# Two attention units' value products and output projections in one run, every second step, in a two-layer graph attention kernel

## The reference

```
# layer 0 (8 heads of 32)
nx = ln(x); q, k, v = nx @ wq + bq, nx @ wk + bk, nx @ wv + bv
scores = q k^T / sqrt(32) + where(adj > 0, 0.1 * adj * adj, -inf)
out = softmax(scores) v                       # the value products
x1 = x + (out @ wo + bo)                      # the output projection
y = x1 + gelu(ln(x1) @ w1 + b1) @ w2 + b2
# layer 1
q, k, v = y @ Wq + bq, y @ Wk + bk, y @ Wv + bv
attn = softmax(where(adj == 0, -inf, q k^T / sqrt(32)))
h = attn v @ Wo + bo
out = ln(h + y) * gamma + beta
```

## Time and profile before

| | |
|---|---|
| median of 3 runs | 2196.2 us (2194.52 to 2197.47) |
| the profiled execution, its own time | 2197.36 us |
| its span, first to last instruction | 2195.3 us |
| TensorE busy | 98% of the span |
| VectorE, ScalarE, GpSimd busy | 82%, 77%, 53% |
| mean granted TensorE clock | 0.988 |

### The profile page before, as it was taken

The page is one execution under the profiler, slowest core; times in us unless marked ns, Lnnn a source line. Parts: engine busy times, 40 slices in busy tenths (PEclk is TensorE's granted clock), DMA queues, the critical chain, the costliest instruction groups (busy, mean ns, idle before and its releaser), DMA issues.

```text
span 2195.3 us, 58908 instructions
## 1 busy us (share of the span) xinstructions
PE 2150.0 (98%) x20300; PEld 1859.5 (85%) x20300; DVE 1802.1 (82%) x8414; ACT 1683.8 (77%) x5646; POOL 1155.7 (53%) x1266
## 2 busy tenths in 40 slices
PE   8899999999999999999999999999999999999986
PEld 6688888888888888888888888888888888888875
DVE  6688888888888888888888888888888888888774
ACT  5578787778777778877778877788877787877773
POOL 4345655445655455655455555455555455555454
PEclk9999999999999999999999999999999999999997
DMA  4010111011111001111101110101111001110000
GB/s 128 25 35 28 40 33 40 23 31 35 40 33 36 27 28 38 37 36 31 32 28 38 34 39 31 33 26 40 33 40 31 30 28 40 33 40 29 22 14 17
DMA packets 94309, 75.74 MB, mean 35 GB/s; under 512 B 8129, under 2 KB 93761, under 8 KB 94017
## 3 DMA queue, kind: packets, MB, share of 16 engines
q1 hardware_dynamic: 94016, 71.99, 10.7%
HBM read 55.20 MB, written 16.78 MB: 33 GB/s over the span
## 4 chain that ended last, share of the span: by engine, by line
PE 95%; DVE 2%; issue 1%; ACT 1%; POOL 0%; DMA 0%; SPq 0%; POOLq 0%; DVEq 0%
PE p_bank L1124 67%; PE p_heads L1221 10%; PE p_heads L1208 8%; PE p_bank L1240 7%; PE p_bank L1143 4%; ACT scores L650 1%; DVE normed L883 0%; DVE x_two L768 0%; DVE probs_t L920 0%; ACT normed L661 0%; DMA scores<-in_L_gnn_wk 0%; DVE scores L861 0%; DVE adj_c L814 0%; SPq L440 0%; POOL w_up L374 0%
## 5 line engine op out<-in xcount | busy, mean ns | idle before, releaser
L650 ACT ACTIVATE scores<-scores,negmax 128x128 f32<-128x128 f32 x2048 | 793.7, 393 | 25.4 <-DVE negmax L861 25.0
L585 POOL TENSOR_TENSOR scores<-scores,inverse 128x512 f32<-128x512 f32 x512 | 541.9, 1064 | 339.6 <-DVE inverse L872 339.6
L650 ACT ACTIVATION_READ_ACCUMULATOR scores<-scores,negmax 128x1 f32 x2048 | 392.2, 192 | 0.0
L1124 PEld LDWEIGHTS p_bank<-w_down,hidden 128*128 128x128 f32 x3072 | 374.7, 190 | 8.6 <-issue 6.0
L1124 PE MATMUL p_bank<-w_down,hidden 128*128 128x256 f32 x3072 | 381.8, 284 | 0.0
L1124 PE MATMUL p_bank<-normed,w_up 128*128 128x512 f32 x1536 | 370.3, 397 | 1.9 <-DVE normed L883 1.9
L1124 PEld LDWEIGHTS p_bank<-normed,w_up 128*128 128x128 f32 x1536 | 285.0, 189 | 67.6 <-issue 8.4
L1221 PE MATMUL p_heads<-ident,scores 128*128 128x128 f32 x2048 | 313.1, 276 | 8.3 <-DVE negmax L861 3.5
L861 DVE CUSTOM_DVE_ANT_0 scores<-p_heads,adj_a 128x128 f32<-128x128 f32 x1024 | 235.2, 286 | 43.7 <-issue 43.7
L1221 PEld LDWEIGHTS p_heads<-ident,scores 128*128 128x128 f32 x2048 | 241.2, 141 | 35.0 <-DVE negmax L861 11.1
L673 ACT ACTIVATE p_bank<-p_bank,ready_cols 128x512 f32<-128x512 f32 x256 | 169.5, 662 | 131.4 <-PE p_bank L1124 125.9
(11 more groups left out here) (117 smaller groups left out, 3704.5 us busy)
## 6 DMA issues: line engine op xcount, KB each, us to landing
res_a<-in_x SPq DMA_DIRECT2D x32, 512.0 KB, 3.8
out<-res_c SPq DMA_DIRECT2D x128, 128.0 KB, 1.7
x_in<-in_x SPq DMA_DIRECT2D x31, 512.0 KB, 3.8
adj_a<-in_adj SPq DMA_DIRECT2D x32, 256.0 KB, 2.9
adj_c<-in_adj SPq DMA_DIRECT2D x32, 256.0 KB, 2.9
piece_room<-in_L_gnn_w SPq DMA_DIRECT2D x2, 512.0 KB, 8.1
x_two<-in_x SPq DMA_DIRECT2D x1, 512.0 KB, 5.5
res_c<-in_L_gnn_w SPq DMA_DIRECT2D x1, 512.0 KB, 6.3
```

What stands on the lines that cost most here:

```text
L585: nc.gpsimd.tensor_tensor(rows_g, rows_g, inverse[:, step % 2, heads].unsqueeze(2).broadcast_to([P, HC, P]), ALU.mult).then_inc(probs_made, 1)
L650: last = nc.scalar.activation(scores[:, k % 2, h], scores[:, k % 2, h], ACT.Exp, scale=-1.0, bias=negmax[:, k % 2, h:h + 1], accum_out=tot ...
L1124: last = nc.tensor.matmul(dst, stationary(i), moving(j), start=(n == 0), stop=(n == total_n - 1))
```

## The change

V and W are made for two units at once, in the odd steps: step 1 takes the last two A units of the turn before, step 3 the first two C units, step 5 the last two C units, step 7 the first two A units. Even steps have no V and no W. `probs_t` and `heads_t` get two rooms each. The two units' evacuations are one instruction of double width (`heads_high`, `heads_low`, `add_residual`); `measure` takes two units with shared steps. Q, K and V are moved so that even steps have more of them. The norm of stage M's input is applied for units 0 and 1 in steps 0 and 1, for units 2 and 3 in step 2. The steps after the change:

The order within a step is the same as before on each engine. The core of the diff:

```
-        by_step[k] = ([("V", r - 2), ("W", r - 2)] if r >= 2 or pending else []) + (
+        pair = [(r - 3, r - 2)] if r % 2 and (r >= 3 or pending) else []
+        by_step[k] = [("V", units) for units in pair] + [("W", units) for units in pair] + (
             [("T", r - 1)] if r >= 1 or pending else [])
...
-        early = {1: ("Q", "A", 0), 2: ("V", "A", 0), 4: ("DOWN", 1), 6: ("Q", "C", 0), 7: ("V", "C", 0)}
+        early = {1: ("Q", "A", 1), 2: ("V", "A", 0), 4: ("DOWN", 1), 6: ("Q", "C", 0), 7: ("V", "C", 1)}
         mid = {0: [("K", "A", 0)], 3: [("UP", 0), ("UP", 1)], 5: [("K", "C", 0)]}
-        fill = {0: [("K", "A", 1)], 1: [("Q", "A", 1)], 2: [("V", "A", 1)],
+        fill = {0: [("K", "A", 1), ("Q", "A", 0)], 2: [("V", "A", 1)],
                 3: [("UP", j) for j in range(2, FC)] + [("DOWN", 0)],
-                5: [("K", "C", 1)], 6: [("Q", "C", 1)], 7: [("V", "C", 1)]}
+                5: [("K", "C", 1)], 6: [("Q", "C", 1), ("V", "C", 0)]}
...
-        probs_t = sb("probs_t", [P, H, P])
-        heads_t = sb("heads_t", [P, 2, KC, P], F32R)
+        probs_t = sb("probs_t", [P, 2, H, P])
+        heads_t = sb("heads_t", [P, 2, 2, KC, P], F32R)
...
-                nc.vector.tensor_tensor(x[:, b, :], p_bank[bank][:, 0:D], x[:, b, :], ALU.add
-                                        ).then_inc(drained[bank], 1)
+                x = residual[stage][:, b:b + len(units), :].rearrange("p g n -> p (g n)")
+                nc.vector.tensor_tensor(x, p_bank[bank][:, 0:len(units) * D], x, ALU.add).then_inc(drained[bank], 1)
...
-                    if k == 2:
-                        for r in s.late.get(k, []):
-                            apply_norm(t, r, GB - 1)
+                    if k == 2 and s.m and s.pending:
+                        normalize_m(t, 2, t.group_m, t.projections("A", 1))
+                        normalize_m(t, 3, t.group_m, t.projections("A", 1))
...
+            def value_products(t, units):
+
+                bank, dst = take(t, ("O", units))
+                u_last, stage, _ = t.unit(units[-1])
+                pe.wait_ge(turned_out0, u_last + 1)
+                pe.wait_ge(turned_out1, u_last + 1)
...
+                for i, r in enumerate(units):
+                    _, _, b = t.unit(r)
+                    for h in range(H):
+
+                        j, c = h % HC, h // HC
+                        last = nc.tensor.matmul(dst[HD * j:HD * (j + 1), (i * KC + c) * P:(i * KC + c + 1) * P],
+                                                values[room(t, stage)][:, b, h * HD:(h + 1) * HD],
+                                                probs_t[:, parity(r), slot_of(c, j), :], start=True, stop=True)
+                last.then_inc(filled[bank], 1)
+
+            def project(t, units):
+
+                bank, number = t.bank(("O", units))
+                pe.wait_ge(drained[bank], number)
+                bank, dst = take(t, ("W", units))
+                w = weight[weights_of[t.unit(units[0])[1]][3]]
+                for at_unit in range(len(units)):
+                    last = three_passes(dst[:, at_unit * D:(at_unit + 1) * D], [
+                        (lambda i, c=c: heads_t[:, i, at_unit, c, :], lambda j, c=c: w[:, j, c, :])
+                        for c in range(KC)])
+                last.then_inc(filled[bank], 1)
```

More of the change, by code:

```diff
@@ L135, in __init__ @@
             self.high0 = before.high0 + before.turns * len(before.high)
+            self.projected0 = {stage: before.projected0[stage] + before.turns * len(before.projected[stage])
+                               for stage in "AC"}
         assert not self.looped or len(self.use) % BANKS == 0
     def number(self, ops):
+        for op in only("W", ops):
+            stage, _ = self.order[op[1][0]] if op[1][0] >= 0 else self.before.order[op[1][0]]
+            self.projected[stage][op[1]] = len(self.projected[stage])
         for use in [use for op in ops for use in bank_uses(op)]:
@@ L195, in bank, with projections, projection @@
         return n % BANKS, self.grown(n // BANKS + 1, len(s.use) // BANKS)
+    def projections(self, stage, more):
+        return self.grown(self.s.projected0[stage] + more, len(self.s.projected[stage]))
+    def projection(self, units):
+        stage = self.unit(units[0])[1]
+        return self.projections(stage, self.s.projected[stage][units])
     def normed_room(self, what):
@@ L551, in rstd_of @@
             def rstd_of(t, ops):
[L552 to L555, removed]
+                for _, units in only("W", ops):
+                    _, stage, b = t.unit(units[0])
+                    make_rstd("M" if stage == "A" else "C", b, b + len(units), t.projection(units) * 3 + 3)
             def add_bias(stage, sem, count, first, pairs):
@@ L599, in body @@
                         make_probs(k, 0)
-                    for r in s.late.get(k, []):
-                        finish(t, r)
+                    for units in s.late.get(k, []):
+                        for r in units:
+                            finish(t, r)
                     if k == 3 and s.m:
@@ new lines, in measure, with finish_c @@
+            def measure(t, units):
+                _, stage, b = t.unit(units[0])
+                bank, number = t.bank(("W", units))
+                dve.wait_ge(drained[bank], number)
+                layer_norm_steps("M" if stage == "A" else "C", residual[stage], b, b + len(units),
+                                 t.projection(units) * 3)
+            def finish_c(t, units):
+                if t.unit(units[0])[1] == "C":
+                    for r in units:
+                        b = t.unit(r)[2]
+                        normalize("C", res_c, res_c, b, b + 1, t.projection(units) + 1)
@@ L1227, in lagging @@
+            def lagging(t, op, which):
                 if op == "T":
                     for g in range(2):
-                        turn(t, r, g)
+                        turn(t, which, g)
                 if op == "V":
-                    bank, dst = take(t, ("O", r))
-                    pe.wait_ge(turned_out0, u + 1)
-                    pe.wait_ge(turned_out1, u + 1)
-                    if b == 0:
-                        for i in range(2):
-                            pe.wait_ge(*drained_bank(*made(t, "V", stage, i)))
@@ L1237, in lagging @@
[L1237 to L1251 removed]
+                    value_products(t, which)
```

108 lines of the change are left out of this document (44 added, 64 removed).

## The result

The kernel with the change takes **2347.4 us** (median of 6 runs, 2345.8 to 2351.6) against 2197.7 us before (6 runs, 2194.5 to 2202.7): ratio 1.068, 95% interval 1.067 to 1.070. It is slower by 150 us. The prediction was 2308, range 2248 to 2362. The profiled execution's span went from 2195.3 to 2344.8 us, +149.5. Its mean granted TensorE clock is 0.988, as before.

A forecast was written before the change was run, and what follows sets the result against it. TensorE's stream was taken to bound each turn: 4.24 us lost less 0.52 saved is +3.72 us a turn, +112 us over 30 turns, giving 2308 us. Range 2248 to 2362; this case's own 2280 to 2337.

The forecast's parts named there:

- rival A: Whole turn: TensorE's clock also falls near the idle pieces; one fall a turn gives 2350 us, two 2392; chance 0.17.
- The saving: TensorE's stream: pairing V saves form changes, 0.13 us a pair, 0.52 us a turn (0 to 0.88).
- Wait 1: Steps 0, 2, 6: half 1 of the transposes, due at 2.58, waits for probabilities ready at 3.01: 0.43 us.
- Wait 2: Scores of step 2 and of step 0 wait for VectorE's copy: 1.07 us and 0.20 us lost.
- Wait 3: Step 0: VectorE late, starting at 2.14 instead of 0.80; transposes' half 1 at 4.35: 1.77 us lost, Wait 1 included.
- Step 2: Masks 0.14 late, transposes' half 1 at 3.15, 0.57 us lost; plus 0.2 at XT M for norms: 0.77 in all.
- Step 4: The 5.9 us of DOWN 1 stand ahead of the transposes' half 1 and nothing waits.
- The turns at the ends: Turns outside the 30 full ones: counted as nothing, a few us either way.
- B: Step 0: VectorE isn't late, its queue runs 1.3 us ahead of the count; 1.84 us a turn, 2251 us; chance 0.13.
- C: Whole kernel faster: probabilities come in time, no wait arises, only the saving is left; 2180 us; chance 0.04.
- D: Whole kernel the same: saved and lost cancel or TensorE's stream doesn't change, within 0.2%; chance 0.02.

The follow-up runs named there:

- e12: Changed kernel with pairs for C units only, Q, K, V in old places, inversion first, C norms behind the copy, res_a load before two stores: 2214.6 us, ratio 1.009.
- e6: Changed kernel with Q, K, V in old places, inversion first, C norms and step 0's M norm behind the copy, res_a load before two stores: 2212.2 us, ratio 1.007.
- e4: Changed kernel with VectorE inverting the previous unit's sums before masking half 0 of the next: 2326.9 us, ratio 1.059.
- e2: Kernel before with only the new places of Q, K and V, V and W still one unit a step: 2245.6 us, ratio 1.021.
- e3: Changed kernel with step 4's two C norms moved on VectorE from ahead of x_in's norms to behind the copy of T: 2351.8 us, ratio 1.070.
- e5: Changed kernel with step 4's C norms behind the copy and the res_a load issued ahead of two stores: 2316.5 us, ratio 1.054.
- e11: Changed kernel with GpSimd's finishing of step 4's C units held until VectorE has normed x_in, and res_a's load before two stores: 2314.5 us, ratio 1.053.
- e9: Changed kernel with VectorE's copy of T half 1 put ahead of the double add_residual: 2404.8 us, ratio 1.094.
- e7: Kernel before with inversion first, norms behind the copy, and res_a's load ahead of two stores: 2217.2 us, ratio 1.009.

## Why the prediction was right, and where it was not

The forecast's case came true, in its mechanism and in the steps that it names; its size was short by 38 us of span (149.5 against 112). The 2347.4 us lie outside 2280 to 2337, the range that the prediction gave for this case alone. They lie inside 2248 to 2362 only because its upper part was left for rival A, the clock, which is not what happened: that the range holds is partly luck. So is it that A with one fall a turn gives 2350.

**The saving: right.** V of two units takes 1102.66 - 1101.65 = 1.01 us, as 0.57 + 0.44 foresaw, and scores without V go to the next piece in 0.66 us (1078.12 to 1078.78). e12 measures it with what waits are left: 0.27 us for two pairs. e6 gives 66.11 - (66.33 - 0.83) = 0.6 us a turn without its waits, for a forecast of 0.52. The sentence of the Trainium skill on the drain, which the prediction cites (TensorEngine Tiling), stands there under Key Properties; the trace agrees as far as a second unit's V in the same form costs 0.44 us and the first 0.57.

**Wait 1: right.** Half 1 of T in step 6 comes at 1097.66 - 1094.62 = 3.04 (forecast 3.01). e4 shows that the product behind the inversion sets it.

**Wait 2: right.** Scores of step 2 wait 1.04 us (forecast 1.07), those of step 0 wait 0.16 (forecast 0.20). The copy ahead of the latter starts at 1106.86 - 1100.99 = 5.87 (forecast 5.82). e2, which has 0.87 us of the first wait without any pair, shows that the moved products are its main cause.

**Wait 3: right.** VectorE's queue runs as counted: in step 0 the first mask starts at 1109.80 - 1107.69 = 2.11 (forecast 2.14), and half 1 of T comes at 1112.04 - 1107.69 = 4.35 (forecast 4.35):

```profile
1106.86 0.68 DVE L946 COPY probs_t<-p_heads 128x512 f32<-128x512 f32 x1
...
1109.80 0.28 DVE L887 CUSTOM_DVE_ANT_0 scores<-p_heads,adj_c 128x128 f32<-128x128 f32 x1
```

**Step 2: right but for 0.2 us.** Half 1 comes at 1125.20 - 1122.05 = 3.15, as forecast. The 0.2 us at XT M did not come: no wait stands there in the trace. It was near, since in e4, where half 1 comes sooner, XT M waits for the norms.

**Step 4: this is the step that failed.** The prediction said "In step 4 the 5.9 us of DOWN 1 stand ahead and nothing waits." That was looked at for half 1 of T, which indeed does not wait. It was not asked for XT C, whose second half needs VectorE's evacuation of DOWN 1. Taking V (0.57) and W's 0.71 out of the step brings XT nearer by 1.28 us: with no wait the step is 9.71 - 1.28 = 8.43 long, and e3, e5 and e11 have it at 8.42. The step took 9.55, 1.13 us more, 33 us over 29 turns. The second norm of C stands ahead of `x_two` on VectorE, at 1.05 us where 0.4 is its own length. Of GpSimd's two finishing pairs the prediction said only that they take 3 us and that the next probabilities are due later; that they lengthen VectorE's norms in this step was not in it. e5 and e11 each take the loss away (31 and 33 us). With this term the sum would have been 112 + 33 = 145 us, 2341 us.

**"The turns at the ends count as nothing": off by 7 us.** They cost 0.9 us ahead and 6.5 us behind the full turns. Of the 6.5, steps 0 to 2 of turn 32, which has no Q, K and V left, hold 3.2 us (19.22 against 16.03), and the last turn 3.8 us (40.9 against 37.1); the rest of turn 32 is 0.5 us shorter. In steps 0 to 2 of turn 32 the clock was lower than before. Windows over them, before and after (columns as in the earlier trace rows):

```profile
2097.37:2113.40 16.03, 11.94 (x147) 9.76 (x147) 13.69 (x83) 11.77 (x53) 10.66 (x12) 0.89 0.01 2
```

```profile
2240.36:2259.58 19.22, 12.39 (x125) 9.55 (x125) 13.14 (x81) 11.74 (x53) 10.18 (x10) 0.78 0.00 0
```

An estimate from these windows: 0.22 x 19.2 = 4.2 us of clock are missing after, 0.11 x 16.0 = 1.8 before, so up to 2.5 of the 6.5 us may be the clock. Which wait of these turns costs how much was not tried apart.

112 + 33 + 7, less some 2 us for XT M and small differences of the other steps, is the 150 us measured.

**The rivals.** A, the clock: in the full turns it did not fall. The window of step 0 shows a granted clock of 1.00 with waits of 1.01 and 0.56 us in it, and a window over all 30 full turns (115.65 to 2240.36) shows 1.00 as well. Steps 0 to 2 of turn 32, above, ran lower than before; the mean stayed 0.988. The Trainium skill (TensorE: Matmul & The Clock Gate, HAM oscillation) tells of a kernel that falls to half clock between its bursts, over waits longer than any in these turns; to let it speak for two falls a turn here stretched the page, and the trace shows none. A fall was not far, though: in e9, with a wait of 1.74 us at the same place, the clock was 0.82 over 9.27 us in one of the 8 turns with a fall, so part of it at 1.2 GHz instead of 2.4, and such a step was 0.87 us longer. In the other 22 full turns the same wait brought no fall. B, VectorE not late: out by the 2.11 and the 1.01. C and D, faster or the same: out; e6 shows that even with most waits removed the saving of 0.6 us a turn is smaller than the 0.8 us that is left of them, and in e12 the wait of step 7 alone (0.76 us) is more than its two pairs save.

**What stays open.** The waits that keep e6 above the kernel before were not removed one by one. If step 7 of e12 took its old 6.64, its turn would be 65.83 and the kernel, by an estimate, some 6 us faster than before (8 us over 30 turns, less what e12 loses at the ends); GpSimd's finishing work would have to move for that, and no such kernel was run. e11 holds the load order of e5 as well as its own edit; that the order has no part in step 4 is argued from e3, which reaches 8.42 without it.

## What to carry to other kernels

A piece of work that is taken out of a full queue is also cover for every consumer behind it in the step: list all of these with the time that each producer is ready, not only the one whose margin was known. Here the pairs saved some 0.15 us each and took 1.28 us of cover from each even step. When two pieces of a second engine's work are put together, look at what a third engine does beside them: a duration read from a quieter place may not hold there. A reordering that helps one step moves the others (e3, e7, e9): the next thing in each in-order queue, DMA queues too, is to be followed before it is called free.

## What the runs showed of the hardware

In this kernel VectorE's norms are held up by GpSimd's work, and by the times below for a whole instruction at a time. The lengths of single instructions in step 4 (ns, minimum/median/maximum), first in the kernel after, then in e11:

```profile
L794 DVE TENSOR_SCALAR res_c<-res_c,moments_C,rstd_C x2: 383/756/1128, 1081.3 to 1081.6; 128x256 f32<-128x256 f32 x2
...
L794 DVE TENSOR_SCALAR x_in<-x_in,moments_A,rstd_A x4: 821/858/894, 1082.7 to 1085.0; 128x256 f32<-128x256 f32 x4
```

```profile
L796 DVE TENSOR_SCALAR x_in<-x_in,moments_A,rstd_A x4: 397/401/402, 1071.4 to 1072.3; 128x256 f32<-128x256 f32 x4
```

And GpSimd beside the first of them, in the kernel after:

```profile
1081.49 1.12 POOL L609 TENSOR_TENSOR scores<-scores,inverse 128x512 f32<-128x512 f32 x1
1082.57 0.79 POOL L596 TENSOR_TENSOR res_c<-res_c,gamma 128x256 f32<-128x256 f32 x1
```

The first norm of C started before GpSimd's product and took 0.383 us. The second started near 1081.6, inside the product, and took 1.128 us: it ended at 1081.32 + 1.43 = 1082.75, 0.14 us after the product's end at 1082.61. The four norms of `x_in` then took turns with GpSimd's four finishing instructions, 0.82 to 0.89 us each, where each takes 0.40 us when GpSimd is quiet. That GpSimd is the cause is shown for `x_in` by e11; for the norm of C it is read from the times alone. The hold by the product is not new: in the kernel before it is the first norm of `x_in` that starts inside it and takes 1.132 us, and in e5 likewise one takes 1.131 us. New in the changed kernel are one more norm, 0.4 us, and four finishing instructions beside `x_in` in place of two. Together the queue of norms grew from 3.32 us (1147.99 to 1151.31) to 4.54 us (1081.32 to 1085.86). The Trainium skill (SBUF — State Buffer, Who interferes with whom) says that a `tensor_scalar` in a two-port mode and a GpSimd instruction shut each other out, whichever issues first holding the ports for its whole length. The trace agrees, with the 1.128 against 0.383 us.
